# Cross attention on one core: a softmax shift in 64-row tiles, later keeping of results, and a new order of VectorE's and TensorE's steps

## The reference, cut to what matters

```python
x = x + xattn(layernorm(x), ctx, ctx)      # x (32, 56, 128), ctx (32, 1500, 128)
#   q = x1 Wq^T + bq ; k = ctx Wk^T + bk ; v = ctx Wv^T + bv
#   softmax(q k^T) v
x = x + ffn(layernorm(x))                  # heads, gates, top 2 of 8 experts
```

## Time and profile before

| | us |
|---|---|
| median of 3 runs | 552.55 (550.83 to 552.56) |
| the profiled execution | 552.02 |
| its span on the core | 550.0 |
| attention pairs, first to last step | about 45 to 216 |
| feed-forward part | about 228 to 550 |

### The profile page before, as it was taken

The page is one execution under the profiler, slowest core; times in us unless marked ns, Lnnn a source line. Parts: engine busy times, 40 slices in busy tenths (PEclk is TensorE's granted clock), DMA queues, the critical chain, the costliest instruction groups (busy, mean ns, idle before and its releaser), DMA issues.

```text
span 550.0 us, 25189 instructions
## 1 busy us (share of the span) xinstructions
PE 437.6 (80%) x10768; PEld 366.0 (67%) x10768; DVE 468.2 (85%) x850; ACT 293.3 (53%) x400; POOL 143.1 (26%) x125
## 2 busy tenths in 40 slices
PE   1466889889988998658887888788888888887864
PEld 0245777777777877547776776677676767676754
DVE  2987778887888895579999999999999999999962
ACT  1254756766675674425544554555555455545631
POOL 8262767775777685000000000000000000000000
PEclk9987999999999999678999999999999999999996
DMA  7814443454345300000000000000000000000000
GB/s 175 265 40 133 137 155 116 135 182 141 114 161 177 120 1 4 1 1 3 8 3 4 4 4 0 4 4 2 2 4 4 0 4 4 4 0 4 7 7 5
DMA packets 18124, 29.44 MB, mean 54 GB/s; under 512 B 2988, under 2 KB 13996, under 8 KB 18092
## 3 DMA queue, kind: packets, MB, share of 16 engines
q1 hardware_dynamic: 18092, 28.97, 16.9%
HBM read 28.05 MB, written 0.92 MB: 53 GB/s over the span
## 4 chain that ended last, share of the span: by engine, by line
DVE 43%; PE 33%; issue 14%; ACT 6%; DVEq 1%; DMA 1%; SPq 1%; POOL 1%; ACTq 0%; POOLq 0%
DVE ctxf_all L856 8%; PE ps L958 6%; PE ps L1201 5%; DVE ctxf_all L827 5%; DVE rs L844 3%; PE ps L989 3%; DVE ctxT L653 3%; DVE ah L874 2%; DVE attnf L866 2%; ACT ah L557 2%; PE ps L1004 2%; PE ps L1005 2%; PE ps L1006 2%; PE ps L1014 2%; PE ps L1126 1%
## 5 line engine op out<-in xcount | busy, mean ns | idle before, releaser
L369 POOL TENSOR_TENSOR nat<-ctxf_all,nat 128x640 f16<-128x640 f32 x32 | 70.6, 2223 | 50.1 <-ACT nat L442 50.1
L958 PE MATMUL ps<-ident,nat 128*128 128x128 f16 x768 | 60.9, 225 | 10.0 <-DVE ctxT L653 5.2
L442 ACT CAST nat<-ctxf_all 128x1536 f16<-128x1536 f32 x32 | 45.5, 1470 | 39.2 <-PE ps L1006 39.2
L856 DVE TENSOR_TENSOR ctxf_all<-mixp,diag_h 128x3584 f16<-128x3584 f16 x32 | 63.2, 2014 | 0.0
L958 PEld LDWEIGHTS ps<-ident,nat 128*128 128x128 f16 x768 | 46.2, 100 | 23.4 <-issue 13.0
L1098 PE MATMUL ps<-xn,mT 128*128 128x112 f16 x256 | 41.9, 218 | 11.2 <-DVE mixp L851 11.2
L375 POOL TENSOR_TENSOR p<-pf,p 128x672 f16<-128x672 f32 x32 | 46.1, 1460 | 12.8 <-ACT pf L455 12.8
L653 DVE COPY ctxT<-ps 128x1024 f16<-128x1024 f16 x64 | 42.7, 685 | 4.7 <-PE ps L958 4.7
L1201 PE MATMUL ps<-ctxf_all,ah 128*64 128x112 f16 x1024 | 29.6, 219 | 18.5 <-DVE ah L874 18.4
L447 ACT COPY ctxT<-ps 128x1024 f16<-128x1024 f16 x32 | 33.0, 1033 | 20.3 <-PE ps L958 20.3
L973 PE MATMUL ps<-qk_cur,ctxT 128*128 128x56 f16 x384 | 33.5, 188 | 12.6 <-DVE ctxT L653 10.7
(11 more groups left out here) (169 smaller groups left out, 1288.3 us busy)
## 6 DMA issues: line engine op xcount, KB each, us to landing
ctxf_all<-in_ctx_dram SPq DMA_DIRECT2D x32, 704.0 KB
ctxf_all<-in_ctx_dram SPq DMA_DIRECT2D x32, 46.0 KB
x_all<-in_x_dram SPq DMA_DIRECT2D x2, 448.0 KB
out_dram<-y_all SPq DMA_DIRECT2D x32, 28.0 KB
ctxf_all<-in_ctx_dram SPq DMA_DIRECT2D x32, 18.0 KB
fwq_nat<-in_L_ffn_Wq_dram SPq DMA_DIRECT2D x1, 512.0 KB, 9.2
fwk_nat<-in_L_ffn_Wk_dram SPq DMA_DIRECT2D x1, 512.0 KB, 9.6
fwv_nat<-in_L_ffn_Wv_dram SPq DMA_DIRECT2D x1, 256.0 KB, 5.8
```

Source lines behind the costliest of these rows:

```text
L369: pool.tensor_tensor(nat[k][:, 1, 7 * C:], ctxf[k][:, 7 * C:], nat[k][:, 0, 7 * C:], ALU.subtract).then_inc(natlo2, 1)
L442: act.copy(nat[k][:, 0, :], ctxf[k][:, :]).then_inc(nathi, 1)
L856: last = dve.tensor_tensor(dv[:, part, :, :, :], mixp[:, part, :, :].unsqueeze(2).broadcast_to((P, 2 * NQ, HALF, H)), diag_h[:, :, :].unsq ...
L958: last = pe.transpose(ps[:, (3 * b + c) % 2, :].bitcast(F16)[:, P * (j % 8):P * (j % 8) + P], nat[k][:, j // TK, C * (j % TK):C * (j % TK) ...
```

## The change

Five edits, all in the steps of the pairs:

- DVE: `shifts` ends after the high part of dg. The rest of dg moves to `shift_rest`, behind split1 and behind `den_out`. `sums_out` and `den_out` change places, and `den_out` gets the wait for `dend`.
- DVE: `moments` comes behind the last copy and loses line 701; `bn_aggr` gets a wait for `mvd`.
- POOL: `keep` also copies the moments to mv_all. It is called for pair-2 ahead of `low_probs`, not for pair-1 behind it.
- PE: one `shift` for both sequences, made of eight matmuls with 64 rows (of weights and of dg) that alternate between the two sequences, in place of twice four with 128 rows. `rows_of` is 0 outside those 64 rows.
- PE: the shift comes behind two turns (first and middle third of n+2) and `project` comes two turns later.

```diff
@@ pool
+                after(pool, mvc, pair + 1)
+                pool.tensor_copy(mv_all[:, bass.ds(pair * 2, 2)], mv_cur[:, :]).then_inc(mvd, 1)
                         queries(pair + 1, 1 - s)
+                    if not isinstance(pair, int) or pair > 1:
+                        keep(pair - 2)
                     low_probs(n, 0, pair)
                     low_probs(n + 1, 1, pair)
-                    if not first:
-                        keep(pair - 1)
@@ vector
                 dve.tensor_scalar(dg[:, 0, :], diag_q[:, :], nshift[:, 0:1], None, ALU.mult).then_inc(dghi, 1)
+
+            def shift_rest(pair):
                 dve.wait_ge(dghi, pair + 1)
                 dve.scalar_tensor_tensor(dg[:, 1, :], diag_q[:, :], nshift[:, 0:1], dg[:, 0, :],
                                          op0=ALU.mult, op1=ALU.subtract).then_inc(dgr, 1)
             def den_out(pair):
+                after(dve, dend, pair + 1)
                 dve.reciprocal(rden[:, :], ps[:, 6, P:P + 1]).then_inc(rdn, 1)
+                after(dve, mvd, pair)
                 dve.bn_aggr(mv_cur[:, :], bst[:, :]).then_inc(mvc, 1)
-                dve.wait_ge(mvc, pair + 1)
-                dve.tensor_copy(mv_all[:, bass.ds(pair * 2, 2)], mv_cur[:, :]).then_inc(mvd, 1)
                         split_lo(n + 2, (2 * s + 2) % 4)
                     if not first:
-                        sums_out(pair - 1)
+                        den_out(pair - 1)
+                    shift_rest(pair)
                     if more:
                         t_evac(n + 2, 0, 0)
                     if not first:
-                        den_out(pair - 1)
+                        sums_out(pair - 1)
                     if more:
                         split_lo(n + 3, (2 * s + 3) % 4)
                         t_evac(n + 2, 0, 2)
                         t_evac(n + 3, 1, 0)
                     if not first:
                         result(pair - 1)
-                        moments(pair - 1)
                     if more:
                         t_evac(n + 3, 1, 2)
+                    if not first:
+                        moments(pair - 1)
@@ tensor
-            def shift(n, pair, b):
+            def shift(pair):
+                pe.wait_ge(c_zero, 10)
                 after(pe, dgr, pair + 1)
                 for a in range(2):
                     for part in range(2):
-                        last = pe.matmul(o, rows_of[:, b, :],
-                                         dg[:, part, :].unsqueeze(1).broadcast_to((P, 6, S)),
-                                         start=False, stop=(part == 1), skip_group_check=True)
-                last.then_inc(shd, 1)
+                        for b in range(2):
+                            r = slice(SLOT * b, SLOT * b + SLOT)
+                            o = ps[:, 2 + 2 * b + a, 0:6 * S].rearrange("p (t q) -> p t q", t=6)
+                            last = pe.matmul(o, rows_of[r, b, :], dg[r, part, :].unsqueeze(1).broadcast_to((SLOT, 6, S)),
+                                             start=False, stop=(part == 1), skip_group_check=True)
+                last.then_inc(shd, 2)
                         turn(n + 2, 0, k0, (0,))
-                    shift(n, pair, 0)
+                        turn(n + 2, 0, k0, (1,))
+                    shift(pair)
                     if more:
-                        turn(n + 2, 0, k0, (1,))
-                    shift(n + 1, pair, 1)
+                        turn(n + 2, 0, k0, (2,))
+                        turn(n + 3, 1, k1, (0,))
                     if not first:
                         project(pair - 1)
                     if more:
-                        turn(n + 2, 0, k0, (2,))
-                        turn(n + 3, 1, k1, (0,))
                         turn(n + 3, 1, k1, (1,))
                         turn(n + 3, 1, k1, (2,))
```

More of the change, by code:

```diff
@@ L390, in steps @@
                     n = 2 * pair
-                    first = isinstance(pair, int) and pair == 0
                     more = not (isinstance(pair, int) and pair == NP - 1)
@@ L413, in _ @@
             steps(NP // 2 - 1)
+            keep(NP - 2)
             keep(NP - 1)
@@ L981, in max_turn @@
                 pe.transpose(ps[:, 7, 0:P], tmax[:, :, :].rearrange("p b q -> p (b q)"), ident[:, :]).then_inc(tmT, 1)
-            def shift(n, pair, b):
+            def shift(pair):
+                pe.wait_ge(c_zero, 10)
                 after(pe, dgr, pair + 1)
                 for a in range(2):
-                    o = ps[:, 2 + 2 * b + a, 0:6 * S].rearrange("p (t q) -> p t q", t=6)
                     for part in range(2):
-                        last = pe.matmul(o, rows_of[:, b, :],
-                                         dg[:, part, :].unsqueeze(1).broadcast_to((P, 6, S)),
-                                         start=False, stop=(part == 1), skip_group_check=True)
-                last.then_inc(shd, 1)
+                        for b in range(2):
[4 more added lines that the diff above has]
+                last.then_inc(shd, 2)
             def values(n, pair, b, k):
```

## The result

The changed kernel takes 558.65 us in the median against 552.55, a ratio of 1.0113 (95% interval 1.0084 to 1.0141): slower by 1.1%, a small loss but clear of 1. One of its four runs took 821.26 us, in a slow state whose cause isn't known; it counts in the median but not in the ratio, and the other three took 558.10 to 558.84. In a second series, five rounds on one chip, it was 559.76 against 551.74, 1.0125 (1.0099 to 1.0152). The profiled execution took 558.46 us with a span of 556.7.

A forecast was written before the change was run, and what follows sets the result against it. It took a cycle through DVE and POOL's alternation, low_probs, line 701 and the last copy as the bound. 552.02 us plus 14 x 0.43 = 6.0 and 0.6 gave 558.6, median 559.0; own range 556.5 to 563, 8-in-10 range 544 to 563.

The forecast's parts named there:

- What bounds it: Steps of the pairs: a cycle through values, split_hi, DVE and POOL's turns, low_probs, line 701, last copy, scores; 10.82 us.
- The rest of dg: DVE, behind split1: with two SBUF inputs it is held to the end of POOL's first low_rows, near 1.3 us, not 0.28.
- X: The start of DVE's split1 in a step, from which the prediction counts its times, in us.
- The price per step: Each step of the pairs: the last copy starts later than X+6.23, at X+6.65 to X+6.83, so +0.42 to +0.60 us.
- The hand-over of 0.24 us: PE's last turn follows the second t_evac by 0.06 or 0.24 us.
- The sum: Pairs 1 to 14: 14 x 0.43 = 6.0 us, pair 0 nothing, last pair +0.6; profiled execution 558.6 us.
- the last pair: No split1 as cover there, the shift comes behind den_out and the rest of dg: once, some +0.6 us.
- The wait for `dend`: den_out on DVE waits for PE's denominator: zero in the steps; in the last pair dend lets DVE go at 213.54.
- The freed last copy: DVE's last copy no longer waits for low_probs through line 701 and could start at X+5.45: a gain of 0.78 us.
- The rival for that: POOL takes the first turn, ahead of split1: +1.2 us a step, 570 us; chance 6%.
- The shift and the tiles: PE: shift starts X+2.53, ends X+3.2 or X+3.8, so exponentials start there, not X+2.97; hidden by 0.3 to 0.6 us.
- The rule on the port pair: VectorE with two SBUF inputs and GpSimd reading SBUF exclude each other for the whole instruction; 4.69 us for 0.39.

The follow-up runs named there:

- Experiment 5: The kernel before with only the moments' part: POOL copies them, keep two pairs late and ahead of low_probs, moments behind the last copy; 550.08 us, ratio 0.9976.
- Experiments 3: The changed kernel with diag_q copied once to PSUM and read there, so the rest of dg has one SBUF input; 543.65 us, ratio 0.9853.
- 6: The changed kernel with POOL's low_rows made to wait for the rest of dg, both operands in SBUF; 550.79 us, ratio 0.9984.
- experiment 1: The changed kernel with the rest of dg put back ahead of split1; 553.88 us, ratio 1.0033.
- experiment 2: The kernel before with only the rest of dg moved behind split1; 588.37 us, ratio 1.0689.

## Why the prediction was right, point by point

**What bounds it.** Right: the alternation of DVE and POOL, not the sum of DVE's work. Experiment 5 shows it from the other side: with line 701 off DVE, its short steps take 10.33 us instead of 10.85, though the copy is worth only 0.17 us of DVE's work.

**The rest of dg.** Right in mechanism and nearly in every time. Expected: it ends X+2.46, low2 X+3.73, split2 X+4.67, the two t_evac X+5.93, the last copy X+6.65 to X+6.83. Measured (X=129.13): X+2.42, X+3.71, X+4.66, X+5.85, X+6.57. Experiments 3 and 6 show the cause by its two halves: with one operand out of SBUF, or with POOL out of the way, it takes 0.26 us.

**The price per step** was the term that was off: about 0.35 us instead of 0.42 to 0.60. The hand-over of 0.24 us to PE's last turn that I kept as the upper end isn't there when t_evac alone is waited for: the last two turns are one record of 1.22 us, from 134.44 (0.05 behind the first t_evac) to 135.66, where two turns without a gap take 1.07, so the last one starts within about 0.1 of the end of the second t_evac (134.98). The steps stretched to 11.2 and not to 11.25 to 11.4.

**What made up for it.** The sum charged 14 steps. The first of them, pair 1, lost nothing: its last copy comes 6.64 us behind split1 instead of 6.24, but split1 itself starts 0.36 earlier. From there to the last one (68.10 to 213.86, before 68.06 to 208.82) 13 steps lost 5.0 us, of which 0.5 is a single step of 11.71 us, in which the granted clock fell to 0.76. I had no term for the clock.

```profile
106.00:112.00 6.00, 4.84 (x65) 3.90 (x63) 5.59 (x9) 4.64 (x7) 5.70 (x6) 0.76 0.32 109
...
219.28 0.17 DVE L689 RECIPROCAL rden<-ps 128x1 f32<-128x1 f32 x1 [0.68 <-PE ps L1023]
```

And the last pair cost 1.1 us, not 0.6: from the last copy to the first normalisation are 20.44 us instead of 19.34. The wait for `dend` is there as worked out (DVE idle 0.68, in the second row above), but the maximum of that pair came 0.75 us later too, behind a gap of 0.8 us in PE's values that the profile puts down to issue; that part is not explained. The feed-forward part adds 0.6. So it was luck that the sum, 558.6 for the profiled execution, met 558.46 so closely: a price per step that was about 0.08 too high (0.43 was used) and charged once too often, and terms that I had left out, cancelled. The direction and the mechanism don't hang on this.

**The freed last copy** was priced at a gain of 0.78 us by DVE's side alone, which was beside the point for the changed kernel but misled experiment 1: a shorter step changes who comes first at split1. The rival for that had been written for the changed kernel only, where it doesn't occur (DVE is idle 0.22 us and 0.05 ahead).

**The shift and the tiles.** Hidden, as predicted; the exponentials start at X+3.35, inside X+3.2 to X+3.8. That the tiles run side by side agrees with the Trainium skill, "TensorEngine Tiling (Array Packing)", section "Key Properties". Of the drain that the same section gives for a change of tiling mode, the trace bounds only the one behind the shift, since PE is idle 0.61 us ahead of it: no more than 0.12 us (0.68 us for eight matmuls where 0.56 is the bare pace of the two tiles together).

**The rule on the port pair** in the Trainium skill, "SBUF — State Buffer", section "Who interferes with whom", agrees with the durations read here, and now also for a scalar_tensor_tensor: two SBUF inputs 1.33 us, one 0.26, at the same place.

## What to carry to other kernels

Before a short VectorE instruction is moved, look at what GpSimd does at its new place and count the instruction's SBUF inputs: a 0.28 us instruction with two of them can cost 1 us, and one operand put in PSUM takes it out of the contest. A tiny instruction with a long record (0.76 us for two numbers) is a waiting instruction; look for a GpSimd record that ends with it, since the chain of waits doesn't name it. And where two engines take turns, work out who arrives first after the change, too: a step that gets shorter may hand the first turn to the other one.

## What the runs showed that was not expected

The turns can settle into an alternation of two steps, one short (10.3 us) and one long (11.4), each setting up the other (experiments 1 and 5), so that a mean step of 10.9 us is no step that occurs. And in experiment 2, where PE waits 1.69 us ahead of the shift in each step, its granted clock was 0.83 in whole stretches of 10 us, and a loss of 1.3 us a step became one of up to 3.7. Not every step with this wait lost the clock, and what decides which do isn't shown.
